# Two heads' narrow scores in one PSUM bank and one exponential, with a new order of the work within a step

## What is computed

```python
attn = jnp.einsum('bqhd,bkhd->bhqk', q, k) * scale
mask = jnp.triu(jnp.ones((S, S), dtype=bool), k=1)
attn = jnp.where(mask[None, None], -1000000000.0, attn)
attn = jax.nn.softmax(attn, axis=-1)
out = jnp.einsum('bhqk,bkhd->bqhd', attn, v).reshape(B, S, D)
```

## Time and profile before

| | before |
|---|---|
| median of 3 runs | 912.02 us |
| the profiled execution | 911.43 us, span 909.6 us |
| TensorE matmul busy, whole span | 864.2 us (95%) |
| VectorE busy | 610.5 us (67%) |
| ScalarE busy | 528.3 us (58%) |
| GpSimd busy | 315.2 us (35%) |
| mean granted TensorE clock | 0.987 of full speed |

### The profile page before, as it was taken

One profiled execution on the slowest core, in us unless ns is written; L12 is line 12 of the kernel. 1 busy time (PEld: TensorE's weight loads), 2 busy tenths in 40 slices (PEclk: granted clock), 3 DMA queues, 4 the chain that ended last, 5 costly groups with the idle time before them and its releaser, 6 DMA issues. The chain is left out here.

```text
span 909.6 us, 20371 instructions
## 1 busy us (share of the span) xinstructions
PE 864.2 (95%) x6607; PEld 515.2 (57%) x6656; DVE 610.5 (67%) x1147; ACT 528.3 (58%) x1312; POOL 315.2 (35%) x465
## 2 busy tenths in 40 slices
PE   6999959999999999999999988999999999999995
PEld 4555423333333333333333322778999999999994
DVE  5888999888888888888888811786533433333332
ACT  4667437777878877787877786334333333333330
POOL 9999653333232233223233331336111111111111
PEclk9999979999999999999999999999999999999998
DMA  7588533422312222111223120847655555555550
GB/s 274 174 233 255 172 115 132 163 71 68 91 43 70 71 71 71 47 45 55 72 71 121 45 94 1 273 143 240 209 176 184 175 181 188 192 176 174 184 168 1
DMA packets 54114, 120.30 MB, mean 132 GB/s; under 512 B 9753, under 2 KB 37018, under 8 KB 47770
## 3 DMA queue, kind: packets, MB, share of 16 engines
q1 hardware_dynamic: 49482, 101.97, 35.9%
q0 software_dynamic: 4560, 17.39, 5.2%
HBM read 96.16 MB, written 23.17 MB: 131 GB/s over the span
## 5 line engine op out<-in xcount | busy, mean ns | idle before, releaser
L804 ACT ACTIVATE arena<-ps_pair 128x512 f32<-128x512 f32 (+3 forms) x768 | 328.9, 493 | 99.9 <-PE ps_pair L1136 93.0
L893 DVE TENSOR_REDUCE B_block_max<-ps_item 128x8 f32<-128x1024 f32 x288 | 340.6, 1221 | 38.5 <-PE ps_item L1043 35.0
L1136 PE MATMUL ps_pair<-q_stack,k_stack 99*128 99x512 bf16 (+5 forms) x720 | 182.4, 330 | 12.5 <-ACT arena L804 7.6
L719 POOL TENSOR_SCALAR_AFFINE_SELECT arena<-arena 128x256 f32<-128x256 f32 x256 | 103.9, 407 | 202.6 <-ACT arena L804 200.2
L1152 PE MATMUL ps_pair<-arena,B_v_quad 128*32 128x512 f32 (+3 forms) x1536 | 163.6, 498 | 1.0 <-ACT B_oacc L818 0.7
L1136 PEld LDWEIGHTS ps_pair<-q_stack,k_stack 99*128 99x128 bf16 (+1 forms) x768 | 54.0, 97 | 187.8 <-ACT arena L804 170.8
L1748 PEld LDWEIGHTS C_bank<-arena 128*128 128x128 f32 x1248 | 145.5, 192 | 3.3 <-ACT arena L1415 1.3
L1748 PE MATMUL C_bank<-arena 128*128 128x128 f32 x1248 | 145.9, 275 | 1.0 <-ACT arena L1415 1.0
L1767 PE MATMUL C_ps_p<-arena 128*128 x624 | 141.1, 379 | 0.0
L1401 ACT ACTIVATE arena<-C_bank,ffn_columns 128x128 f32<-128x128 f32 x156 | 44.6, 368 | 143.0 <-PE C_bank L1748 143.0
L1767 PEld LDWEIGHTS C_ps_p<-arena 128*128 128x128 f32 x624 | 115.6, 190 | 14.3 <-issue 0.2
(11 more groups left out here) (171 smaller groups left out, 726.3 us busy)
## 6 DMA issues: line engine op xcount, KB each, us to landing
arena<-in_w_exp SPq DMA_DIRECT2D x39, 1024.0 KB, 5.0
qk_parts<-arena SPq DMA_DIRECT2D x32, 384.0 KB, 3.5
q_stack<-qk_parts SPq DMA_DIRECT2D x96, 128.0 KB, 2.9
k_stack<-qk_parts SPq DMA_DIRECT2D x64, 128.0 KB, 2.9
arena<-in_w_exp POOLq DMA_DIRECT2D x8, 1024.0 KB, 6.3
rows<-payload SPq DMA_DIRECT2D x39, 130.5 KB, 2.1
arena<-in_x SPq DMA_DIRECT2D x8, 512.0 KB, 4.6
arena<-in_x_feat SPq DMA_DIRECT2D x8, 512.0 KB, 5.8
```

The source lines that it names most:

```text
L719: pool.affine_select(out=block_p, in_=block_p, compare_op=ALU.is_ge, fill=0.0, base=0, pattern=[[0, 2], [1, P]], channel_multiplier=-1).th ...
L804: act.activation(pr[s % PR][:, h, 0:QW - off], ps_s[(QH * s + j) % R][:, 0:QW - off], ACT.Exp, scale=scale).then_inc(s_e, 1)
L893: dve.tensor_reduce(bmx[:, g:QH:GH, first:first + 3 * gap + 1:gap], src[:, :, :].rearrange("p c (b n) -> p c b n", n=P), AX.X, ALU.max).th ...
L1136: pe.matmul(ps_s[(QH * s + j) % R][:, 0:QW - off], ks[rows, r, half, bass.ds(g * SEQ + kb * P, P)], qs[rows, r, half, bass.ds(g * SEQ + c ...
```

## The change

A table `SHARE` says 2 for pieces of 256 and 128 columns and 1 for the others. In those pieces the scores of two heads (0 and 2, then 1 and 3) go side by side into one bank, and one exponential reads both and writes to the two heads' rows. A step has 40 exponentials in place of 48; all waits on their semaphore count so. TensorE waits for a free bank only ahead of the first score of a bank. Three banks remain. The order is new too: gaps of the items, the maxima's transpose and the PV blocks, the place of the copy out of `ps_o`, and the place of GpSimd's three operations.

```diff
-        MAX_AT, OUT_AT = 5, 46
-        ITEM_AT = (0, 3, 6, 8, 8, 13, 13, 18, 20, 20, 27, 27, 30, 32, 35, 37, 37, 43)
-        PV_AT = ((3, 2), (6, 2), (11, 2), (15, 2), (18, 2), (23, 2), (27, 2), (31, 2), (35, 2), (39, 2), (43, 2), (47, 2))
-        EVAC = 1
-        NM_AT = 1
+        MAX_AT, OUT_AT = 3, 46
+        ITEM_AT = (0, 5, 6, 9, 9, 14, 14, 18, 23, 23, 26, 28, 31, 31, 37, 41, 44, 44)
+        PV_AT = ((2, 2), (6, 2), (11, 2), (14, 2), (18, 2), (23, 2), (28, 3), (28, 2), (35, 2), (41, 3), (44, 3), (44, 2))
+        SHARE = [2 if off >= 2 * P else 1 for _, _, off in subs]
+        exps = [QH // n for n in SHARE]
+        exps_to = [sum(exps[:k]) for k in range(SUB + 1)]
+        EXPS = exps_to[SUB]
+
+        def score_bank(Q, s, j):
+
+            W, n = QW - subs[s][2], SHARE[s]
+            return ps_s[(EXPS * Q.const + exps_to[s] + j // n) % R][:, j % n * W:(j % n + 1) * W]
+
+        EVAC = 0
+        NM_AT = 0
...
-                                wait(pool, s_e, Q, QH * SUB, QH * s + 2 * p + 2)
+                                wait(pool, s_e, Q, EXPS, exps_to[s] + (2 * p + 2) // SHARE[s])
...
-                        for j, h in enumerate(HEAD_ORDER):
-                            if j == 0:
-
-                                wait(act, s_pv, Q, SUB, s + 1 - PR)
-                            wait(act, s_s, Q, QH * SUB, QH * s + j + 1)
-                            act.activation(pr[s % PR][:, h, 0:QW - off], ps_s[(QH * s + j) % R][:, 0:QW - off],
+                        W, n = QW - off, SHARE[s]
+
+                        wait(act, s_pv, Q, SUB, s + 1 - PR)
+                        for u in range(exps[s]):
+                            h = HEAD_ORDER[n * u]
+                            wait(act, s_s, Q, QH * SUB, QH * s + n * (u + 1))
+                            act.activation(pr[s % PR][:, h:h + 2 * n - 1:2, 0:W],
+                                           ps_s[(EXPS * Q.const + exps_to[s] + u) % R][:, 0:n * W].rearrange("p (h n) -> p h n", h=n),
                                            ACT.Exp, scale=scale).then_inc(s_e, 1)
...
-                    wait(pe, s_e, Q, QH * SUB, QH * s + j + 1 - R)
+                    if j % SHARE[s] == 0:
+                        wait(pe, s_e, Q, EXPS, exps_to[s] + j // SHARE[s] + 1 - R)
                     rows = slice(0, SROWS[0] + MROWS if half == 0 else P)
-                    pe.matmul(ps_s[(QH * s + j) % R][:, 0:QW - off], ks[rows, r, half, bass.ds(g * SEQ + kb * P, P)],
+                    pe.matmul(score_bank(Q, s, j), ks[rows, r, half, bass.ds(g * SEQ + kb * P, P)],
...
-                    wait(pe, s_e, Q, QH * SUB, QH * s + QH)
+                    wait(pe, s_e, Q, EXPS, exps_to[s + 1])
```

## The result

The changed kernel takes 929.04 us (median of 5 runs, 924.95 to 931.06) against 912.02 (911.74 to 913.37). The ratio is 1.018, with a 95% interval of 1.016 to 1.019: it is 1.8% slower. The forecast was 901.7, in a range of 895.5 to 910.5. The profiled execution took 924.95 us (span 923.1). It is the fastest of the five, 4.1 us under their median, and 13.5 more than the profiled one before. All of the 13.5 lies in the attention; no trace shows the rest of the medians' 17.0.

A forecast was written before the change was run, and what follows sets the result against it. TensorE was taken to bound the full step, nearly without a stall. Savings 14 x 0.55 + 1.8 + 0.8 = 10.3 us took the profiled 911.43 to 901.1, or 901.7 on the median; range 895.5 to 910.5.

The forecast's parts named there:

- The other moves: Copy out of `ps_o` straight behind its PV block, piece buffers, GpSimd's operations: TensorE does not wait, 0 us.
- No DMA is moved: DMA loads, under the moves priced at nothing: none is moved by the change, 0 us.
- The slow rival: Gaps 28 and 44: late item delays PV, copy, exponentials, fourth score; 917 us at w = 0.9; chance 0.13.
- w: Wait for VectorE of an item ahead of PV blocks, gaps 28 and 44; costs w - 0.35 above 0.35, twice a step.
- The sum for the new order: TensorE in a full step: 21.5 us of scores, PV, items and transposes, plus 43 changes of kind at 0.11 us.
- The rival in which ScalarE paces: Full steps: the ring of three banks sets the distances, each step gains 1.05 us, 894.7 in all; chance 0.13.
- the rival in which VectorE paces: Full steps: VectorE's handovers with two buffers can't be shortened, only the last steps gain, 909.4 us; chance 0.12.
- the 0.55 of five changes: TensorE in a full step: 43 changes of kind in place of 48, 5 x 0.11 = 0.55 us less.
- the 0.46 us that the prediction set at nothing: TensorE stalls in a full step that could go: at most 26.86 - 26.40 = 0.46 us, taken as 0.
- beside TensorE, nothing in a full step: Paired exponentials: 1.05 us less ScalarE a step, counting directly only where TensorE has slack.
- The step without items: Step 15, where ScalarE leads: 1.05 us of exponentials plus 0.7 of idle time, 1.8 us gained.
- the tail: Half step behind step 15, holding one of the two narrow stretches: 0.8 us gained.

## Why the prediction was wrong

**The step that failed is "The other moves": "I take 0".** I looked up one of the copy's two waits, the one for the PV block. The code has the second right below it in `evac`: `if present(Q, OUTT) is not None: wait_full(act, Q, OUTT)`. With `EVAC` at 1 the first half's copy came behind gap 47, past `OUTT` in gap 46, and the wait never showed in the trace: the earlier trace rows say one wait in 32, for another instruction. A wait that is always met leaves no row. Moving the copy four gaps ahead made it bind: 1.73 us of ScalarE and 1.02 of TensorE in gap 47. A full interval takes 27.37 us with it and 26.04 without it, 1.3 us in each of thirteen, 17 us.

**"No DMA is moved" failed too.** No line with a DMA moved, but the loads of the weights stand in GpSimd's stream behind the last mask of the step before, and that mask waits for exponentials that the new order brings sooner. The margin to the last stack load was about 0.6 us (half of the row of 1.22 behind 494.34 puts its issue at 494.95, the weights' at 495.54); it became -0.86 (503.27 against 504.13, taken in the same way from the row of 503.52). This cost 8 us of the profile's 13.5, and about 12 by the ratios. A stall of TensorE for 2.2 us was not all of it: from 508 to 511 matmuls were busy only 0.54 us, the granted clock was 0.83 in that stretch and then 0.50, the lower of its two levels (1.2 GHz), to beyond 515, while the step's widest PV block took 1.94 us in place of 1.06. The interval is 4.8 us longer than the eleven, by a wait of 2.2. The other long one is 3.3 longer, by a wait of 1.9. The two steps of the prediction that failed make 17 and 8 us, a little more than the 23.8 by which the profiled execution missed its 901.1.

**The slow rival had the right place and sign, not the releaser.** I priced it as a wait for the PV block behind a late item, with a chance of 0.13. In the changed kernel that part is 0.4 us of ScalarE, at the second half's copy, and TensorE has no wait there; the run with `OUTT` in gap 42 took the rival's path. The rival was also said to decide against the change from w = 0.6. By its own formula 14 x (2 x (w - 0.35) - 0.55) - 2.6 turns positive at w = 0.72.

**What held.** TensorE bounds a full step, and starts of rows price it. The sum for the new order was 21.5 + 43 x 0.11 = 26.2, forecast as 26.3; with both causes gone it took 26.04. Two PV blocks back to back took 0.79 us (340.35 to 341.14) against the 0.82 that one change less gives, so the pairs of PV blocks were counted rightly. ScalarE's busy time went to 20.25 (20.3 said). The rival in which ScalarE paces fell with the pairs in the old order; the rival in which VectorE paces fell with the second buffer, where VectorE is busy 23.25 of 26.04 us and still not the bound. By the Trainium skill's "Perfetto Trace Analysis", section Identifying the Most-Contended Engine, headroom of TensorE is judged by MFU (the share of peak arithmetic) and by the share of weight loads. The prediction left MFU out, and it is not worked out here. By the loads, 38% (10.00 of 26.04), VectorE with its 89% would be first in a step that TensorE fills; here the measurement decides against that measure.

**Part of the hit is luck.** The step fell from 26.86 to 26.04, by 0.82 us, not by the 0.55 of five changes. Before, TensorE had three idle rows of 0.15 to 0.16 us in the full step, the 0.46 us that the prediction set at nothing; with the second buffer there are none. The other 0.36 is less than five changes, and the sum charged changes at `MAXT` that the rows do not show. Here are its rows before the change:

```profile
340.35 0.38 PE L1136 MATMUL ps_pair<-q_stack,k_stack 99*128 99x512 bf16 x1 [0.16 <-issue]
340.57 0.27 PE L1012 MATMUL ps_item<-cst,B_mx 128*96 128x128 f32 x1
340.68 0.38 PE L1136 MATMUL ps_pair<-q_stack,k_stack 128*128 128x512 bf16 x1
```

From start to start the score keeps TensorE 0.22 us and `MAXT` 0.11, where the sum has 0.325 and 0.21. The sum so had about 0.2 too much in both kernels, and in the old one the idle time made up for it.

**Terms mis-sized.** The pairs as "beside TensorE, nothing in a full step" is true of the old order only. In the new one they carry 2.1 us, because TensorE waits for narrow exponentials without them. The step without items gained 0.5 of the 1.8 us forecast, the tail 0.6 of 0.8. The copy's wait for `OUTT` is in the step without items too (1.12 us of ScalarE and 1.02 of TensorE). Where the copy comes late and the PV block stands in gap 3, this step takes what was forecast (22.7):

```profile
530.95:553.77 22.82, 20.75 (x157) 6.64 (x153) 1.05 (x2) 20.03 (x43) 6.40 (x17) 1.00 0.22 87
```

## What to carry to other kernels

Before an instruction is moved ahead, list every wait in its helper, not only those that the trace shows; a wait that is always met is invisible until the move makes it bind. Ask the same of each DMA that sits behind work which becomes faster: it moves without being touched, and where two queues load what is needed soon and what is needed late, tie the late one to the landing of the other rather than to a margin of half a microsecond. When TensorE is the bound, count its changes of kind; but an order that groups its work needs deeper stores on the other side, so order, bank sharing and buffers have to be tried together.

## What was not expected of the hardware

Changing the kind of matmul (rows and columns of the tile) cost about 0.11 us between scores, items and PV blocks, and blocks of one kind behind each other paid it once, the fp32 PV blocks too (0.79 us for two). Around the one-matmul `MAXT` it did not show (0.22 and 0.11 us).

In this kernel two weight loads of 1 MB, issued 0.25 us ahead of two stack loads on another queue, took these from 2.4 us to 6.4 and 6.7 until they had landed.

TensorE stalls of 1.9 and 2.2 us came with a granted clock of 0.50 that outlasted them, and the two intervals became 3.3 and 4.8 us longer.
